# Delaying the transposes and gate matmuls of an attention output loop by two blocks, and moving layer-norm scaling from ScalarE to VectorE

## What is computed

```python
def attn(x):                       # S = 2048, D = 1024
    q, k, v = x @ Wq.T + bq, x @ Wk.T + bk, x @ Wv.T + bv
    weights = softmax(q @ k.T / sqrt(D))
    return einsum('bqk,bqd->bkd', weights, v)   # sums over q

def ffn(x):
    c = top4_of_best_2_groups(softmax(x @ gate_w.T))      # T x 16
    y = sum_e c[:, e] * ((silu(x @ w1[e]) * (x @ w3[e])) @ w2[e])
    return y + (silu(x @ ws1) * (x @ ws3)) @ ws2

x = x + ln(attn(ln(x)))
x = x + ln(ffn(ln(x)))             # ln has no weights, eps 1e-5
```

## Time and profile before

| what | value |
|---|---|
| time of the kernel, median of 2 runs | 5763.85 us (5755.86 and 5771.84) |
| the profiled execution's own time | 5374.42 us |
| its span, first to last instruction, slowest core | 5372.9 us |
| spans of the 8 cores | 5362.1 to 5372.9 us |
| mean granted TensorE clock of the cores | 0.865 to 0.867 |
| first attention output stage (stage 4 of batch row 0) | 497.6 to 990.1 us |
| second one | 3177.0 to 3669.4 us |

### The profile page before, as it was taken

How to read it: one execution, slowest core, us unless ns; L and a number is a source line. 1 busy time by engine, 2 the same in 40 slices (tenths; PEclk the granted TensorE clock), 3 DMA queues, 4 the chain that set the end, 5 groups by cost and what they waited for, 6 DMA issues and landing times.

```text
span 5372.9 us, 52518 instructions; the slowest of 8 cores (5362.1 to 5372.9 us)
## 1 busy us (share of the span) xinstructions
PE 4159.8 (77%) x18864; PEld 1937.1 (36%) x18864; DVE 1758.5 (33%) x2382; ACT 1083.8 (20%) x1490; POOL 280.8 (5%) x150
## 2 busy tenths in 40 slices
PE   4578445499999999999245774545999999999991
PEld 2233222244444444444022332322444444444440
DVE  2222111333333333333522221113333333333336
ACT  3224221211111111111132242122111111111111
POOL 0000000100000000000000000001000000000000
PEclk8788666699999999999667886667999999999995
DMA  3000010321212121220330001003212121221203
GB/s 118 32 8 12 35 36 32 121 79 63 88 54 94 54 88 63 79 83 1 110 129 32 8 12 39 32 32 121 87 55 94 51 91 63 79 79 63 83 1 121
DMA packets 125282, 339.01 MB, mean 63 GB/s; under 512 B 6228, under 2 KB 6228, under 8 KB 125032
## 3 DMA queue, kind: packets, MB, share of 16 engines
q1 hardware_dynamic: 125032, 335.65, 18.1%
HBM read 302.07 MB, written 33.55 MB: 62 GB/s over the span
## 4 chain that ended last, share of the span: by engine, by line
PE 76%; DVE 8%; ACT 6%; issue 5%; DMA 3%; POOL 1%; DVEq 0%; ACTq 0%; SPq 0%; POOLq 0%
PE PS L33 76%; DVE st L33 5%; ACT RK L33 3%; POOL RK L33 1%; DMA RV<-w 1%; DVE RA L33 1%; DVE RV L33 1%; ACT RA L33 1%; DVE RK L33 1%; ACT RV L33 1%; DMA RA<-Wv 1%; ACT RW L33 1%; DMA RA<-Wk 1%; DMA RA<-Wq 1%; ACT st L33 1%
## 5 line engine op out<-in xcount | busy, mean ns | idle before, releaser
L33 PE MATMUL PS<-RQ,RW 128*128 128x512 bf16 x9216 | 2035.5, 382 | 163.7 <-ACT RK L33 152.7
L33 PEld LDWEIGHTS PS<-RQ,RW 128*128 128x128 bf16 x9216 | 904.9, 98 | 1275.6 <-issue 209.7
L33 PE MATMUL PS<-RW,RK 128*128 128x512 bf16 x4608 | 1023.4, 379 | 3.0 <-DVE RK L33 2.7
L33 DVE SCALAR_TENSOR_TENSOR RA<-PS,c_buf,RA 128x1024 f32<-128x1024 f32 x480 | 616.0, 1283 | 1118.7 <-PE PS L33 1118.2
L33 ACT ACTIVATE RK<-PS 128x512 f32<-128x512 f32 (+1 forms) x608 | 365.1, 619 | 2072.9 <-PE PS L33 2072.9
L33 PEld LDWEIGHTS PS<-RW,RK 128*128 128x128 bf16 x4608 | 431.2, 97 | 572.1 <-issue 96.1
L33 DVE TENSOR_TENSOR RK<-RK,PS 128x512 bf16<-128x512 f32 x576 | 396.1, 688 | 645.6 <-PE PS L33 645.4
L33 PE MATMUL PS<-identf,RK 128*128 128x128 f32 x256 | 62.1, 423 | 457.4 <-ACT RK L33 457.4
L33 PE MATMUL PS<-identb,RA 128*128 128x128 bf16 x640 | 75.4, 298 | 397.3 <-ACT RA L33 201.6
L33 ACT CAST RW<-RV 128x2048 bf16<-128x2048 f32 x108 | 204.7, 1896 | 814.2 <-PE PS L33 748.3
L33 POOL CAST RW<-RV 128x2048 bf16<-128x2048 f32 x108 | 204.7, 1896 | 2683.2 <-PE PS L33 2578.6
(11 more groups left out here) (74 smaller groups left out, 1622.2 us busy)
## 6 DMA issues: line engine op xcount, KB each, us to landing
RV<-w SPq DMA_DIRECT2D x192, 1024.0 KB, 6.8
RV<-ws SPq DMA_DIRECT2D x24, 1024.0 KB, 6.6
RA<-x SPq DMA_DIRECT2D x32, 512.0 KB, 3.3
RK<-x SPq DMA_DIRECT2D x32, 512.0 KB, 4.0
x1park<-RK SPq DMA_DIRECT2D x32, 512.0 KB, 2.9
RK<-x1park SPq DMA_DIRECT2D x32, 512.0 KB, 4.0
out<-RV SPq DMA_DIRECT2D x32, 512.0 KB, 2.9
RA<-Wq SPq DMA_DIRECT2D x4, 2048.0 KB, 12.8
```

Source lines behind the costliest of these rows:

```text
L33: self._last = getattr(self.e, name)(*a, **k)
```

## The change

Three things change.

The scale-and-shift of every layer norm, ScalarE's `activation(..., AF.Identity, bias, scale)`, becomes VectorE's `tensor_scalar` with the same two per-row scalars (multiply, add), in `emit_ln` (stages 2, 4 and 7) and in stage 4's first norm (`a3_aap`, folded into `a3_av2`).

The loop over `kb` is cut in two functions. `a3_front` holds `a3_d` to the second norm; `a3_back` holds transposes, evacuation, gate matmuls and the copy of the logits. The new loop emits `a3_front(i)` and then `a3_back(i - 2)`.

`a3_t2` no longer waits for `gevf` of block kb-1 (it keeps the wait for `gevac`, which comes after it).

```diff
@@ emit_ln
             def vb2(v):
                 v.wait(mget(key + "sq"))
-                if eng == "v":
-                    v.reciprocal(rstd, rstd)
-                else:
-                    v.tensor_tensor(out=rstd, in0=onescol[:], in1=rstd,
-                                    op=ALU.divide)
+                v.reciprocal(rstd, rstd)
                 v.wait(v.mark())
                 v.tensor_tensor(out=mrstd, in0=negm, in1=rstd, op=ALU.mult)
-                mput(key + "v2", v.mark())
-            pr.on(eng, vb2)
-
-            def sb2(s):
-                s.wait(mget(key + "v2"))
+                v.wait(v.mark())
                 for m in (pre_s or []):
-                    s.wait(mget(m) if isinstance(m, str) else m)
-                s.activation(dst_ap, src_ap, AF.Identity, bias=mrstd, scale=rstd)
-                mput(key + "ln", s.mark())
-            pr.on("s", sb2)
+                    v.wait(mget(m) if isinstance(m, str) else m)
+                v.tensor_scalar(out=dst_ap, in0=src_ap, scalar1=rstd,
+                                scalar2=mrstd, op0=ALU.mult, op1=ALU.add)
+                mput(key + "ln", v.mark())
+            pr.on("v", vb2)
@@ stage 4
-                for kb in range(QB):
+                def a3_front(kb, b=b):
                     pp = (kb % 2) * 2
...
                         v.tensor_tensor(out=st[:, c0 + 3:c0 + 4], in0=st[:, c0:c0 + 1],
                                         in1=st[:, c0 + 2:c0 + 3], op=ALU.mult)
-                        mput(f"b{b}k{kb}av2", v.mark())
+                        v.wait(v.mark())
+                        v.tensor_scalar(out=lnt[:, (kb % 2) * D:(kb % 2 + 1) * D],
+                                        in0=bank(pp, 2),
+                                        scalar1=st[:, c0 + 2:c0 + 3],
+                                        scalar2=st[:, c0 + 3:c0 + 4],
+                                        op0=ALU.mult, op1=ALU.add)
+                        mput(f"b{b}k{kb}lnev", v.mark())
                     pr.on("v", a3_av2)
-
-                    def a3_aap(s, b=b, kb=kb, pp=pp):
-                        c0 = (4 + kb % 2) * 4
-                        s.wait(mget(f"b{b}k{kb}av2"))
-                        s.activation(lnt[:, (kb % 2) * D:(kb % 2 + 1) * D],
-                                     bank(pp, 2), AF.Identity,
-                                     bias=st[:, c0 + 3:c0 + 4],
-                                     scale=st[:, c0 + 2:c0 + 3])
-                        mput(f"b{b}k{kb}lnev", s.mark())
-                    pr.on("s", a3_aap)
...
+                def a3_back(kb, b=b):
...
                     def a3_t2(t, b=b, kb=kb):
                         t.wait(mget(f"b{b}k{kb}xn2ln"))
                         t.wait(mget(f"b{b}k{kb - 1}gevac"))
-                        t.wait(mget(f"b{b}k{kb - 1}gevf"))
...
+                for i in range(QB + 2):
+                    if i < QB:
+                        a3_front(i)
+                    if 0 <= i - 2 < QB:
+                        a3_back(i - 2)
```

More of the change, by code:

```diff
@@ L216, in emit_ln @@
         def emit_ln(key, src_ap, dst_ap, slot, sq_ap, pre_v=None, pre_s=None,
-                    eng="v"):
+                    out_dt=None):
             c0 = slot * 4
@@ L238, in vb @@
                 mput(key + "vs", v.mark())
-            pr.on(eng, vb)
+            pr.on("v", vb)
             def sb(s):
@@ L651, in build, with a3_av2 @@
                     pr.on("s", a3_as)
-                    def a3_av2(v, b=b, kb=kb):
+                    def a3_av2(v, b=b, kb=kb, pp=pp):
                         c0 = (4 + kb % 2) * 4
@@ L690, in build @@
                     if A3LVL < 2:
-                        continue
+                        return
                     emit_ln(f"b{b}k{kb}x1", x1t[:, (kb % 2) * D:(kb % 2 + 1) * D],
@@ L697, in build @@
                             pre_s=[f"b{b}k{kb - 2}gtr"])
-                    def ren3(b=b, kb=kb):
-                        mput(f"b{b}k{kb}xn2ln", mget(f"b{b}k{kb}x1ln"))
-                    ren3()
+                    mput(f"b{b}k{kb}xn2ln", mget(f"b{b}k{kb}x1ln"))
+                def a3_back(kb, b=b):
                     if A3LVL < 3:
-                        continue
+                        return
                     def a3_t2(t, b=b, kb=kb):
```

## The result

The changed kernel is faster. The median of its 11 runs is 5472.44 us (5166.99 to 5815.02), that of 10 runs of the kernel before 5389.44 us (5373.48 to 5873.11); the ratio is 0.9604, with an interval of 0.9588 to 0.962. In some executions of either kernel the cores of one die, or of both, showed a lower granted clock and took up to 14% longer; the two medians contain such executions, the ratio and the times of the experiments do not. What it compares is 5373.48 to 5391.71 us before and 5166.99 to 5170.84 us after. The first two runs of the kernel before, the 5755.86 and 5771.84 shown ahead of the prediction, are far above this. The profiled executions stand at 5374.42 before and 5170.84 after: 203.6 us less, where the working gave 204. The predicted 5560 (5490 to 5640) misses, though.

What follows compares the result with a forecast made beforehand. Stage 4's loop is bound by one chain through four engines, for which TensorE waits. Savings of 166 (stage 4), 18 (stage 2) and 20 (stage 7) make 204 us: 5763.85 to 5560 us, range 5490 to 5640.

Steps and rivals of the forecast that it cites:

- the sum's last line: Whole kernel: the 389 us between profile and run median stays, so 204 comes off 5763.85, giving 5560 us.
- Stage 4: Delay by two blocks shortens the loop from 30.73 to 26.51 us; 166 us saved over both batch rows.
- the third item: Stage 4 loop, end of second root to first copy: 4.40 us becomes 0.10, the only item leaving the loop.
- what stands ahead matters by 0.2: Stage 4 matmul groups: block 0, with other work ahead, took 9.93, so 9.7 us per group was kept.
- Scaling from PSUM: Stage 4's first norm: scaling stays on the chain, moves from ScalarE to VectorE, and costs +0.08 us per block.
- Scaling from SBUF: Norms on VectorE: 0.71 us per scaling, between 0.6 and 1.28, against 1.24 on ScalarE.
- Stage 7: Closing norm: scaling on VectorE saves 0.63 us per tile, 32 tiles, 20 us.
- it just fits: Stage 7's reload: 5.7 us from add start to landing, against a new period of 6.0.
- A: Stage 4: copies of kb-2 get ahead of kb's chain, loop 15.1 us, 296 us more saved, 5264; chance 0.04.
- B: Stage 4: TensorE's clock stays at 1.2 GHz through the matmuls; only 90 us saved, 5674; chance 0.06.
- D: Experts' stage loses its high clock, 0.21 us per slow matmul; 5908 at 12% of them; chance 0.03.
- C: Norms don't gain: SBUF scaling 1.28 us, stage 7 reload late; 166 saved, 5598; chance 0.87 together with the forecast.

Runs made afterwards that it cites:

- the kernel with early copies: Changed kernel with copies and casts of block kb-2 put between squares and first root of block kb in ScalarE's row; 4817.39 to 4818.55 us, ratio 0.8925.

## Why the prediction was right in its mechanism and wrong in its number

**The step that failed: the sum's last line, "so I subtract the same 204: 5763.85 - 204 = 5560".** Everything was worked out on the profiled execution, 5374.4, and ended at 5170; the profiled execution after took 5170.84. The prediction then treated the 389 us between the profile and the two runs as a constant that both kernels carry. It is none. The kernel before, run again, took 5373.48 to 5391.71 in six of eight executions (5524.40 and 5873.11 in the others), and the profiled 5374.42 lies among the six. So the 389 us belonged to those two executions and not to the kernel. Of the two, only the times are on record, not the clocks of their cores, so their cause is not shown. The sign was there to be read: two runs 7% above a profile whose own time stands beside its span. The range should have had 5170 in it, as the case that the profile shows the kernel's usual time.

**That 204 met 203.6 is luck.** The terms missed by +17.1 (stage 4), -4.3 (stages 1 to 3), -13.8 (stage 7) and +1.1 (gate and experts), and these cancel. The forecast of the saving is borne out in its main term and its mechanism, not to the microsecond.

**Stage 4: right mechanism, 166 predicted, 182.7 measured.** "Only the third item above leaves it: 4.40 becomes 0.10" holds: the copy starts 0.14 behind the start of the root. Item by item, in the mean of 26 blocks: matmuls to squares 9.31 (predicted 9.92), squares to end of the second root 11.88 (11.76), root to copies -0.06 (0.10), copy to gate 1.32 (1.33), gate 3.40 (3.40): 25.85. In the block of the rows above they are 8.60, 12.03, -0.06, 1.32 and 3.40, 25.29 together. The matmul group is the term that was mis-sized, 9.7 for 9.1. Its row for "what stands ahead matters by 0.2" was one block, the first, and one block does not bound it: later groups of this kernel alone differ by 1.6 us. Over the loops, 25.85 instead of 26.51 is 0.66 x 26 = 17 us, which is the whole miss of this part; start and drain took 66 and 64 us, predicted 65. "Squares to second root" grew from 11.73 in the mean before to 11.88, as much as the scaling from PSUM did.

**Scaling from PSUM: +0.08 predicted, +0.14 measured** (1.344 against 1.20). A per-row pair of scalars costs 0.06 more than the single one of the earlier trace rows. The Trainium skill's "Perfetto Trace Analysis", Optimizing Scalar/DVE Operations, from which the prediction's estimate was +0.29, gives the right sign and twice the size. The estimate leaves out a note of the same section, that a profiled instruction shows about twice this overhead. With it my estimate from the page is 0.96 for ScalarE and 1.32 for VectorE: the trace agrees for VectorE (1.344) and disagrees for ScalarE (1.20).

**Scaling from SBUF: 0.71 predicted, 0.812 measured.** It does run well under the 1.34 of the same form from PSUM, so the tier that the Trainium skill's "VectorE: DVE Perf Modes", The perf-mode tier table, gives to fp32 from SBUF holds for per-row scalars; this trace agrees. With the 0.18 gap ahead of it a norm saves 0.40, not 0.57, so 32 x 0.40 = 12.8; stages 1 to 3 took 13.7 us less, instead of 18.

**Stage 7: 20 predicted, 6.2 measured.** Two terms were off: the saving per tile, 0.40 instead of 0.63, and the step "it just fits". The median landing is 4.1 to 4.4 us by core (4.2 on the slowest), not 4.0, and the reload was late in 11 tiles: 32 x 0.40 = 12.8, less 7.0 of waits, is 5.8. The prediction took the reload's margin from core 6 alone, one of the two cores whose trace before shows no wait for it. The edit that issues the reload earlier removes the waits, but the time moved by 1 us only.

**Rivals.** A (full overlap, 5264) did not come, for the reason given, ScalarE's row; the kernel with early copies shows both halves, since it removes the reason and gets the overlap, with a loop of 13.0 instead of A's 15.1, as gate matmuls and transposes then run at a granted clock of 1.00 (1.93 and 1.04 us) and the groups take 7.07 to 8.75. B and D are refuted: groups got shorter, and gate and experts took the same time to 1 us. C was half true on the slowest core, in stage 7.

## What to carry to other kernels

When a loop is software-pipelined, read every engine's row, not only the one that waits: the stage that is delayed must also stand early in the rows of the engines that serve it. Here the delay and the scalings, with the copies left behind, gave 4%, and four instructions moved within one row another 7%. And where the profiled execution and the median of the runs differ by more than the scatter of the runs, the difference is a case of its own in the range, not a constant to add.

## What the runs showed of the hardware that was not expected

TensorE's granted clock fell in the kernel with early copies although TensorE was seldom idle for more than 2 us. Stretches of 1 us (PE, PEld, DVE, ACT, POOL, granted clock, DMA, GB/s):

```profile
605.00:606.00 1.00, 0.00 (x0) 0.00 (x0) 1.00 (x2) 1.00 (x5) 0.00 (x0) 1.00 0.00 0
606.00:607.00 1.00, 0.69 (x7) 0.72 (x7) 0.79 (x3) 1.00 (x3) 0.00 (x0) 1.00 0.00 0
607.00:608.00 1.00, 1.00 (x12) 1.00 (x12) 0.40 (x3) 0.24 (x2) 0.00 (x0) 1.00 0.00 0
608.00:609.00 1.00, 1.00 (x6) 0.45 (x6) 0.78 (x3) 0.00 (x0) 0.00 (x0) 0.53 0.00 0
...
611.00:612.00 1.00, 1.00 (x5) 0.42 (x4) 0.00 (x0) 0.00 (x0) 1.00 (x1) 0.76 0.00 0
```

The clock stays at 1.00 through transposes, 2.1 us of idling and the gate matmuls, and is 0.53 in the stretch in which the 128x512 matmuls begin (608.13); it is back within four microseconds. The group that it hits takes 8.7 us, its neighbour 7.07. Ahead of the fall TensorE had done 1.04 us of transposes, idled 2.1 and done 1.98 of gate matmuls; the group at 596.25 had much the same ahead of it (1.04, 1.75, 1.93) and stayed at 7.07, and the one at 583.10, with 1.04, 1.66 and 1.93 ahead, took 8.75. So none of the three lengths tells the two kinds of group apart. No run here takes one of them away by itself, and the cause stays open.

The two parts of the change were not additive: 132 and 44 us alone, 204 together. And removing waits of 7 us on the slowest core moved the time by 1 us.
